# A two-layer sequence model: how attention outputs are stored and later loads are issued, how place sums are multiplied, and where the experts' weight remainders are formed

## The reference

```
h = x + attention(rmsnorm(x, ln1_w), wq, wk, wv, wo)      # softmax over 1024 keys, 16 heads
z = rmsnorm(h, ln2_w).reshape(-1, 256)
rw, sel = top_k(z @ gate_w.T, 2);  rw = softmax(rw)
for e in range(8):
    we = sum(where(sel == e, rw, 0))
    out += ((silu(z @ w1[e].T) * (z @ w3[e].T)) @ w2[e].T) * we[:, None]
```

## Time and profile before

| | us |
|---|---|
| median of 3 runs | 3253.65 (3253.13 to 3257.46) |
| profiled execution, its own time | 3254.25 |
| its span, first to last instruction | 3252.5 |

### The profile page before, as it was taken

The page is one execution under the profiler, slowest core; times in us unless marked ns, Lnnn a source line. Parts: engine busy times, 40 slices in busy tenths (PEclk is TensorE's granted clock), DMA queues, the critical chain, the costliest instruction groups (busy, mean ns, idle before and its releaser), DMA issues. The chain is left out here.

```text
span 3252.5 us, 63820 instructions
## 1 busy us (share of the span) xinstructions
PE 2902.9 (89%) x22870; PEld 1817.2 (56%) x22871; DVE 2332.7 (72%) x3875; ACT 1874.9 (58%) x3391; POOL 557.4 (17%) x899
## 2 busy tenths in 40 slices
PE   5888888884999999999999999889769999999970
PEld 4666776663333333333333333357658888888850
DVE  5766666763999999999999999847774444444436
ACT  3555655551588888888888888743223333333320
POOL 1122212221000000000000000001124444444430
PEclk7889999986899999999999999988789999999985
DMA  1223233223222222222222222258421111111129
GB/s 36 100 88 116 103 116 116 94 88 120 59 69 71 69 68 68 68 68 67 68 68 68 68 69 70 72 174 286 144 85 47 50 52 48 50 50 50 50 84 364
DMA packets 195529, 292.64 MB, mean 90 GB/s; under 512 B 31976, under 2 KB 118272, under 8 KB 195344
## 3 DMA queue, kind: packets, MB, share of 16 engines
q1 hardware_dynamic: 156400, 229.16, 22.1%
q0 software_dynamic: 13056, 35.67, 3.3%
q10 hardware_dynamic: 25888, 25.30, 2.3%
HBM read 159.94 MB, written 127.93 MB: 89 GB/s over the span
## 5 line engine op out<-in xcount | busy, mean ns | idle before, releaser
L866 DVE TENSOR_REDUCE b_mxq<-b_p_m 128x1 f32<-128x1024 f32 x1024 | 1222.1, 1222 | 82.4 <-PE b_p_m L889 75.9
L797 ACT ACTIVATE b_probs<-b_p_e 128x512 f32<-128x512 f32 x2048 | 1105.3, 597 | 159.1 <-PE b_p_e L937 50.0
L889 PE MATMUL b_p_m<-b_kst,b_qst 64*128 64x512 f32 x2048 | 766.6, 455 | 27.1 <-DMA b_vst<-v_d 22.8
L937 PE MATMUL b_p_e<-b_qst,b_kst 64*128 64x512 f32 x2048 | 749.2, 445 | 8.8 <-DMA b_qst<-b_nm 8.6
L908 PE MATMUL b_p_o<-b_probs,b_vst 128*32 128x256 f32 x8208 | 643.8, 391 | 0.5 <-ACT b_probs L797 0.4
L937 PEld LDWEIGHTS b_p_e<-b_qst,b_kst 64*128 64x128 f32 x2048 | 317.0, 185 | 429.9 <-ACT b_probs L797 357.9
L1580 ACT ACTIVATE d_act<-d_p_up 128x512 f32<-128x512 f32 x136 | 81.2, 597 | 487.3 <-PE d_p_up L1642 487.3
L889 PEld LDWEIGHTS b_p_m<-b_kst,b_qst 64*128 64x128 f32 x2048 | 321.2, 188 | 57.7 <-DVE b_mxq L866 30.6
L908 PEld LDWEIGHTS b_p_o<-b_probs,b_vst 128*32 128x32 f32 x8208 | 168.3, 108 | 324.9 <-issue 172.5
L1657 PE MATMUL d_p_y<-w2T,d_hT 128*128 x1096 | 258.7, 379 | 0.8 <-ACT d_hT L1574 0.8
L1595 DVE TENSOR_SCALAR d_xh<-d_p_x,d_ln 128x128 fp32r<-128x128 f32 x272 | 82.9, 346 | 238.9 <-PE d_p_x L1636 238.9
(11 more groups left out here) (281 smaller groups left out, 4002.1 us busy)
## 6 DMA issues: line engine op xcount, KB each, us to landing
b_qst<-qk_d SPq DMA_DIRECT2D x384, 64.0 KB
b_kst<-qk_d SPq DMA_DIRECT2D x384, 64.0 KB
x1y_d<-a_x1y SPq DMA_DIRECT2D x32, 512.0 KB, 4.0
qk_d<-a_hi SPq DMA_DIRECT2D x32, 512.0 KB, 2.8
qk_d<-a_lo SPq DMA_DIRECT2D x32, 512.0 KB, 3.5
v_d<-a_v_s SPq DMA_DIRECT2D x16, 1024.0 KB, 6.5
b_vst<-v_d SPq DMA_DIRECT2D x64, 256.0 KB
o_d<-b_oT SPq DMA_DIRECT2D x64, 256.0 KB, 3.2
```

Source lines behind the costliest of these rows:

```text
L797: nc.scalar.activation(probs[(2 * step + e % 4 // 2) % BUFS][:, (e % 2) * 512:(e % 2 + 1) * 512], p_e[(slot(e) if more1 else e) % EB][:], ...
L866: V_.reduce_max(mxq[half][:, h, qt:qt + 1], p_m[j % 2][:], AX.X).then_inc(s["m_red"], 1)
L889: mm(p_m[j % 2][:, kh * 512:(kh + 1) * 512], qst[r][rows(h), qt * P:(qt + 1) * P], kst[r][rows(h), kh * 512:(kh + 1) * 512], start=True, s ...
L937: mm(p_e[u % EB][:], kst[r][rows(h), kt * P:(kt + 1) * P], qst[r][rows(h), a * 512:(a + 1) * 512], start=True, stop=True).then_inc(s["e_ps ...
```

## The change

Four edits in three stages.

1. In stage b the stores of pairs 0 to 62 move from SP to GpSimd. GpSimd waits for ScalarE's copy, issues the store, does its split, waits until the store has landed and counts `o_free`, for which ScalarE waits before it writes a `b_oT` tile again. Only the last store stays on SP.
2. In stage b SP issues the maxima's copy directly behind the 15 loads. The next stage's loads come behind it and are spread: weights in pair 4, attention outputs in pair 12, and two of the 14 sum loads in each of pairs 11, 19, ... 59.
3. In stage c the place sums are products in fp32r of `ones_r`, `lower_r`, and of `cum` and `hot`, which VectorE now writes as fp32r. Two more copies of 128x128 stand at the stage's start on VectorE.
4. In stage r a product of `less` (minus the identity, fp32r) with `up_hi` is added into the bank that still holds the transposed weights, which leaves the remainder there; ScalarE copies it to `up_lo`. GpSimd's and VectorE's subtractions and ScalarE's two plain copies go. `less` is made on VectorE, at the head of its stage, and needs GpSimd's identity.

```
 # stage b, SP
         def body(pair, i, r, more1, more, more3):
             if more3: ... load(pair + 3, (r + 3) % RING)
-            if pair > 0:
-                store(pair)
-            if pair == PAIRS - 5:
-                load_ahead()
-            if pair == PAIRS - 4:
-                load_sums()
             if more1:
                 maxima(...)
+            if pair == 4:
+                load_weights()
+            if pair == 12:
+                load_outputs()
+            if pair % 8 == 3 and pair > 8:
+                load_sums(pair // 8 - 1)
 # stage b, ScalarE
-            if n > 2:
-                act.wait_ge(s[f"o_out{n % 2}"], 16 * ((n - 1) // 2))
+            act.wait_ge(s["o_free"], n + 1)
             nc.scalar.copy(oT[half][:], p_o[:]).then_inc(s["oT_done"], 1)
 # stage b, GpSimd
         def body(pair, i, r, more1, more, more3):
+            if more1:
+                pool.wait_ge(s["oT_done"], pair + 2)
+                g.dma_start(o_rows[pair], oT[(r + 1) % 2][:]).then_inc(s["o_stored"], 16)
             if more:
                 split(pair + 2, r % 2)
+            if more1:
+                pool.wait_ge(s["o_stored"], pair * 16 + 16)
+                pool.sem_inc(s["o_free"], 1)
 # stage c, TensorE
-            mm(p5[:], ones[:], cum[r][:, :, 0:C], start=True, stop=False)
-            mm(p5[:], lower[:], hot[r][:, :, 1:], start=False, stop=True)
+            mm(p5[:], ones_r[:], cum[r][:, :, 0:C], start=True, stop=False)
+            mm(p5[:], lower_r[:], hot[r][:, :, 1:], start=False, stop=True)
 # stage r, ScalarE
+                if j < 4:
+                    nc.scalar.copy(up_hi[:, e, j // 2, j % 2], p_w[j][:]).then_inc(s[f"hi_done{j}"], 1)
...
+            for j in range(4):
+                act.wait_ge(s[f"rest_ps{j}"], e + 1)
+                nc.scalar.copy(up_lo[:, e, j // 2, j % 2], p_w[j][:]).then_inc(s[f"free{j}"], 1)
 # stage r, GpSimd and VectorE
-                g.tensor_tensor(lo_part, lo_part.bitcast(f32), up_hi[:, e, 1, j % 2].bitcast(f32), ALU.subtract)
+        dve.wait_ge(s["id"], 1)
+        V_.tensor_scalar(less[:], ident[:], -1.0, None, ALU.mult).then_inc(s["less_done"], 1)
-                V_.tensor_tensor(up_lo[:, e, 0, j], p_w[j][:], up_hi[:, e, 0, j].bitcast(f32), ALU.subtract)
 # stage r, TensorE
+        def rest(e, b):
+            pe.wait_ge(s[f"hi_done{b}"], e + 1)
+            mm(p_w[b][:], less[:], up_hi[:, e, b // 2, b % 2], start=False, stop=True).then_inc(s[f"rest_ps{b}"], 1)
         for e in range(NE):
             for j in range(3):
                 transposes(e, j)
+            for b in range(4):
+                rest(e, b)
             for i in range(per):
                 column(e * per + i)
```

More of the change, by code:

```diff
@@ L736, in load_ahead, with load_outputs @@
             sp.dma_start(ahead.xy[0][:], ahead.x1y_rows(x1y_d)[0]).then_inc(s["ahead_w"], 16)
-            for k in range(2):
-                sp.wait_ge(s[f"o_out{k}"], 16 * 4)
+        def load_outputs():
+            sp.wait_ge(s["o_stored"], 16 * 8)
             for half in range(2):
@@ L741, in load_ahead, with load_sums @@
                     sp.dma_start(ahead.oin[half][:, k], ahead.o_rows(o_d)[0, half, 8 * k:8 * k + 8, 0:16, :]).then_inc(s["ahead_o"], 16)
[L743 to L748, removed]
+        def load_sums(batch):
+            sp.wait_ge(s["o_stored"], 16 * (8 * batch + 8))
+            for a in range(2):
+                sp.dma_start(den[:, 2 * batch + a], o_sums[batch, a, :, 16, :].rearrange("g (c j) -> g c j", c=8)).then_inc(s["den_in"], 16)
         def body(pair, i, r, more1, more, more3):
@@ L769, in _ @@
                 sp.dma_start(ahead.rd[half][16 * k:16 * k + 16, :].bitcast(f32), rd_d[k, 0, half]).then_inc(s["ahead_o"], 16)
-        store(PAIRS)
+        sp.wait_ge(s["oT_done"], PAIRS + 1)
+        sp.dma_start(o_rows[PAIRS - 1], oT[0][:]).then_inc(s["o_last"], 16)
         sp.wait_ge(s["ahead_w"], 64)
         sp.wait_ge(s["ahead_o"], 128)
-        for k in range(2):
-            sp.wait_ge(s[f"o_out{k}"], 16 * PAIRS // 2)
+        sp.wait_ge(s["o_last"], 16)
     @block.scalar
@@ L851, in _ @@
         dve.sem_inc(s["m_red"], 2)
+        dve.sem_inc(s["o_free"], 3)
         dve.sem_inc(s["hl_done"], 1)
@@ L1023, in output_projection_and_gate @@
     i32 = mybir.dt.int32
-    ones, lower = sb("ones", [P, P]), sb("lower", [P, P])
+    whole, lower = sb("whole", [P, P]), sb("lower", [P, P])
+    ones_r, lower_r = sb("ones_r", [P, P], f32r), sb("lower_r", [P, P], f32r)
     expert_i, expert = sb("expert_i", [P, NE], i32), sb("expert", [P, NE])
@@ L1027, in output_projection_and_gate @@
     chosen = sb("chosen", [P, T, 2])
-    hot, cum = [sb(f"hot{r}", [P, NE, C + 1]) for r in range(2)], [sb(f"cum{r}", [P, NE, C + 1]) for r in range(2)]
+    hot, cum = [sb(f"hot{r}", [P, NE, C + 1], f32r) for r in range(2)], [sb(f"cum{r}", [P, NE, C + 1], f32r) for r in range(2)]
     where = sb("where", [P, NE, C])
@@ L1143, in normalised @@
             V_.tensor_tensor(oT[half][:], oin[half][:], p1[:], ALU.mult).then_inc(s["oT_done"], 1)
-        V_.memset(ones[:], 1.0)
+        V_.memset(whole[:], 1.0)
         normalised(0, 0, 0, False)
@@ L1194, in place @@
             dve.wait_ge(s["slot_ps"], n + 1)
-            V_.tensor_tensor(where[:], p5[:], hot[r][:, :, 1:], ALU.mult).then_inc(s["where_done"], 1)
+            V_.tensor_tensor(where[:], p5[:], hot[r][:, :, 1:].bitcast(f32), ALU.mult).then_inc(s["where_done"], 1)
             dve.wait_ge(s["where_done"], n + 1)
             V_.reduce_sum(slots[:, n * C:(n + 1) * C], where[:].rearrange("p e c -> p c e"), AX.X).then_inc(s["slot_done"], 1)
-        dve.wait_ge(s["iota_done"], 1)
+        dve.wait_ge(s["lower_done"], 1)
+        V_.tensor_copy(ones_r[:], whole[:])
+        V_.tensor_copy(lower_r[:], lower[:])
         V_.tensor_copy(expert[:], expert_i[:]).then_inc(s["start_done"], 1)
@@ L1286, in places @@
                 pe.wait_ge(s["where_done"], n)
-            mm(p5[:], ones[:], cum[r][:, :, 0:C], start=True, stop=False)
-            mm(p5[:], lower[:], hot[r][:, :, 1:], start=False, stop=True).then_inc(s["slot_ps"], 1)
+            mm(p5[:], ones_r[:], cum[r][:, :, 0:C], start=True, stop=False)
+            mm(p5[:], lower_r[:], hot[r][:, :, 1:], start=False, stop=True).then_inc(s["slot_ps"], 1)
         def body(n, half, b, b_next, before, after):
@@ L1473, in transposes @@
                 if e > 0:
[L1474 to L1477, removed]
+                    pe.wait_ge(s[f"free{b}"], e)
                 for i in range(4):
```

36 lines of the change are left out of this document (13 added, 23 removed).

## The result

| | median us | all runs |
|---|---|---|
| before | 3254.44 | 3253.13 to 3257.46 (4) |
| after | 3228.39 | 3222.0, 3224.88, 3231.89, 3232.49 |

The ratio is 0.9917, 95% interval 0.9896 to 0.9938: 0.8% faster, 26 us (by the interval 20 to 34). The forecast was 3228.6. The profiled execution took 3231.89 us, span 3230.2; it is one of the longer two.

The account below looks back on a forecast made before the run. TensorE was taken to bound stages b and c, VectorE stage r. Terms -12.7 + 0 - 3.0 - 9.4 = -25.1 us led from a median of 3253.65 to 3228.6 us; range 3218 to 3242.

Parts of the forecast that it names:

- Edit 2, -12.7 forecast: Stage b: issuing the maxima's copy before other loads removes the excess of two long pairs, 6.5 and 6.2 us.
- The fourth rival: Stage b: moved loads do nothing, the stall being their DMA traffic itself; 12.7 us stay, 3241 us; chance 0.05.
- Edit 1, 0 forecast: Stage b: a store's issue on GpSimd takes 1 us, hidden; cost 0, at most 0.3 us a pair.
- the room: Stage b: how long a store may hold GpSimd before TensorE notices, estimated at 7.5 us.
- The other gains would have been used up: Stage b rival: stores hold GpSimd beyond 7.5 us; at 7.9 the 25 us of gains are gone; chance 0.08, 0.04 slower.
- Edit 3, -3.0 forecast: Stage c: fp32r place sums save 0.22 us at each of 16 places, except fast cycles and last halves; 3.0 us taken.
- a rival with 0.09: Stage c, more than forecast: shorter cycles shift against the clock; five more fast cycles give -8.5 us, 3220; chance 0.09.
- Edit 4, -9.4 forecast: Stage r: remainders left in PSUM make seven gaps 18.7 instead of 28.4 us, -9.7, with +0.3 at the start.
- The wait: Stage r: VectorE waits 2.67 us for TensorE, seven times, including transposes 2.74 and four new products 0.92.
- The start: Stage r's start: VectorE's first cast comes 1.3 us later, `r_hi` gets 1.0 shorter; together +0.3 us.
- GpSimd's part: Stage r: GpSimd's subtractions stretch VectorE's comparisons by 1.70 us an expert, seven times, and `r_hi` by 1.0.
- The first rival, the lower clock: Stage r: transposes and new products at lower clock, stage +8.4 us, kernel 3246; chance 0.12 in part or full.

Follow-up runs that it names:

- maxima_first: Kernel before with the maxima's copy moved ahead of the other loads in SP's queue, loads not spread, stores still on SP; stage b fell by 12.7 us.
- pieces8: Changed kernel with each of GpSimd's 63 stores cut into 8 DMAs of 16 rows; stage b 1282.2 us, as with whole stores.
- pieces16: Changed kernel with each of GpSimd's 63 stores cut into 16 DMAs of 8 rows; a pair took 21.19 us instead of 20.07, seven pairs 25.8 to 26.9.

## Why the prediction was right

*Sum.* -25.1 was forecast, -26 measured. The stages give -12.0 - 5.5 - 9.8 - 0.4 = -27.7, and stage a +5.5. That 5.5 is no effect of the change: over 14 profiled kernels with one and the same stage a it lasted 802.1 to 814.3 us. This alone is enough for a spread of 10 us among executions of one kernel. The mechanisms and their sizes came out, with edit 3 the exception; that the median agrees with the forecast to 0.2 us is luck, with an interval of 14 us around it.

*Edit 2, -12.7 forecast.* Right in cause and size: the order in one queue (maxima_first, -12.7). The changed kernel shows -12.0, since its regular pair is at the upper of the two values. The fourth rival, that the moved loads do nothing because the stall was traffic, is refuted.

*Edit 1, 0 forecast.* Right. ScalarE never waited for `o_free`, and the issue took 0.56 us, for which I had taken 1 from the nearest row; the room is 7.06, not 7.5. The other gains would have been used up at 7.06 + 0.4 = 7.5 us an issue, not at 7.9.

*Edit 3, -3.0 forecast, -4.7 measured* over the two sets of seven kernels (-5.5 between before and after). The instructions were right: 0.22 in a slow cycle, next to nothing in a fast one (8.18 to 8.13). The step that failed is that I took the number of fast cycles for given, and put the gain from it into a rival with 0.09. It comes with the edit each time.

*Edit 4, -9.4 forecast, -9.8 measured.* The wait is 2.53 against 2.67, as the transposes take 2.54 and not 2.74, and the new products 1.00 and not 0.92. The start costs 8.87 - 8.65 = 0.2 (0.3 forecast). GpSimd's part is confirmed by itself: 12.8 measured, and the forecast had 1.70 x 7 + 1.0 = 12.9.

*The first rival, the lower clock.* It did not come: the granted clock was 1.00 over the products right behind 24 transposes. By the rule of the Trainium skill (TensorE: Matmul & The Clock Gate, Part 4) that transposes do not raise the clock, it would have been 0.50 there. The trace does not agree. Column products run ahead of these transposes, but at the start of the stage there are none. There, in the changed kernel, TensorE had run two small products (0.60 us from 2305.86) and then stood idle for 0.75 us:

```profile
2307.21 3.24 PE L1480 MATMUL r_p_w<-r_ident,raw 128*128 128x128 f32 x16 [0.75 <-DVE r_less L1398]
2310.29 1.04 PE L1482 MATMUL r_p_w<-r_ident,raw 128*128 128x128 f32 x8
```

The 16 take 3.24 us, where the same 16 take 1.91 at an expert later, and the eight take 1.04 as later. The granted clock was 0.50 from 2306.6 to 2309.0 and 1.00 from 2310.3 on, and from 2307.21 to that point TensorE did nothing but transposes.

## What to carry to other kernels

- In one in-order queue, put what the next step waits for ahead of what is wanted some time. The bytes in flight cost nothing here; standing behind their issues cost 12.7 us.
- Freeing an engine pays only as far as the next wait lets it. Here work taken off VectorE and GpSimd became a wait for TensorE, and 8 more pairs of tiles for running ahead then gave 18.4 us, twice what the edit gave alone; without the edit they gave 3.8. After taking work away, look at what the freed engine waits for and whether it may run further ahead.
- Where executions differ by more than an edit is worth, compare the edit's own stage by fixed marks over several kernels.

## What the hardware showed that I had not expected

- A DMA issue on GpSimd held it for 0.56 us with 128 rows, 0.52 with 8 and 0.48 with 16: the price is by issue, hardly by rows. Behind each 128 such issues of stage b the next one began 3.1 us late, in pieces8 and pieces16 alike; the profile shows no cause.
- In stage c the projections at the full clock come mostly one in three with a slow cycle of 9.65 us, and one in four or five with 9.87. I can't say from these runs why.
- The regular pair of stage b takes 20.056 or 20.067 us in different executions, at a granted clock of 1.00 in both. It is worth 0.7 us, and what sets it is open: with the stores on SP three kernels of seven have the upper value, with whole stores on GpSimd all five.
- After a wait of TensorE of 4 to 5 us in stage b, the granted clock over the next 5 us was 0.52 (kernel before, pair 60) and 0.64 (pieces16), so such a wait cost more than its own length.
- At the start of stage r the granted clock rose from 0.50 to 1.00 while TensorE ran transposes alone.
